# First layer of a vision tower: values projected ahead of keys in the prologue, and the value transfers of the first two tiles issued from two queues

## The reference, cut to what matters

```
h = concat([cls_tok, tok(x)])
n = layernorm(h)
q, k, v = heads(n @ Wq.T) * 16**-0.5, heads(n @ Wk.T), heads(n @ Wv.T)
s = q @ k.T
attn = where(causal, 1 + s + 0.5 * s * s, 0)
h = h + merge(attn @ v / (sum(attn) + 1e-6)) @ Wo.T
```

## Time and profile before

| What | Value |
|---|---|
| Median of 3 runs | 276.23 us |
| Profiled execution | 275.67 us |
| Its span, first to last instruction | 273.9 us |
| PE busy | 240.9 us, 88% |
| PE weight loads busy | 189.0 us, 69% |
| DVE busy | 176.6 us, 64% |
| ACT busy | 135.0 us, 49% |
| POOL busy | 130.3 us, 48% |
| Granted TensorE clock | 1.000 over the whole span |

### The profile page before, as it was taken

How to read it: one execution, slowest core, us unless ns; L and a number is a source line. 1 busy time by engine, 2 the same in 40 slices (tenths; PEclk the granted TensorE clock), 3 DMA queues, 4 the chain that set the end, 5 groups by cost and what they waited for, 6 DMA issues and landing times.

```text
span 273.9 us, 8794 instructions
## 1 busy us (share of the span) xinstructions
PE 240.9 (88%) x3644; PEld 189.0 (69%) x3644; DVE 176.6 (64%) x347; ACT 135.0 (49%) x300; POOL 130.3 (48%) x218
## 2 busy tenths in 40 slices
PE   0779989969999899998897999999999997988983
PEld 0667878857787688887686888789988884443331
DVE  0534537621567899999997998898777776435111
ACT  1322011146576566664455566675766554823450
POOL 7331433561042737565587766878654561154000
PEclk9999999999999999999999999999999999999999
DMA  5989650000111011111100000000000000002021
GB/s 165 221 229 304 131 133 0 4 0 30 47 43 35 31 36 38 35 36 36 33 11 0 2 2 2 2 5 6 2 0 2 5 2 0 4 0 68 2 68 45
DMA packets 12541, 12.44 MB, mean 45 GB/s; under 512 B 4435, under 2 KB 11670, under 8 KB 12502
## 3 DMA queue, kind: packets, MB, share of 16 engines
q1 hardware_dynamic: 12086, 11.88, 15.5%
q10 hardware_dynamic: 416, 0.01, 0.1%
HBM read 8.07 MB, written 1.25 MB: 34 GB/s over the span
## 4 chain that ended last, share of the span: by engine, by line
PE 63%; DVE 18%; issue 7%; DMA 5%; ACT 4%; SPq 2%; DVEq 0%; ACTq 0%
PE psum L1261 12%; PE psum L1297 9%; PE psum L1458 5%; PE psum L1441 5%; DMA img<-in_x 4%; PE psum L1541 3%; PE psum L1604 3%; PE psum L1592 3%; DVE img L1024 3%; PE psum L1516 3%; PE psum L1376 2%; PE psum L1531 2%; PE psum L1233 2%; DVE big L1016 2%; PE psum L1574 2%
## 5 line engine op out<-in xcount | busy, mean ns | idle before, releaser
L481 POOL TENSOR_SCALAR ve<-mvs 114x1 f32<-114x1 f32 x44 | 17.0, 387 | 81.1 <-DVE mvs L979 80.2
L1297 PE MATMUL psum<-hnT,a 128*128 128x114 f32 x352 | 49.0, 282 | 1.1 <-issue 0.6
L1297 PEld LDWEIGHTS psum<-hnT,a 128*128 128x128 f32 x352 | 43.1, 191 | 6.7 <-ACT img L702 2.6
L1261 PE MATMUL psum<-wT,patchT 128*114 128x256 f32 x132 | 33.0, 404 | 1.6 <-DVE patchT L933 0.8
L476 POOL TENSOR_SCALAR big<-mT,parmask 128x228 f32<-128x228 f32 x22 | 22.3, 1026 | 18.4 <-ACT mT L671 18.4
L482 POOL TENSOR_TENSOR rstd<-ve,nhalf 114x1 f32<-114x1 f32 x44 | 28.2, 641 | 3.7
L1261 PEld LDWEIGHTS psum<-wT,patchT 128*114 128x114 f32 x132 | 24.3, 190 | 7.0 <-DVE patchT L933 2.1
L1016 DVE SCALAR_TENSOR_TENSOR big<-big,img 76x912 f32<-76x912 f32 x11 | 15.8, 1438 | 13.1 <-ACT big L727 12.9
L977 DVE BATCH_NORM_STATS2 st<-h_all 114x6 f32<-114x256 f32 x44 | 18.8, 428 | 1.5
L1024 DVE RECIPROCAL img<-img 128x228 f32<-128x228 f32 x11 | 17.3, 1570 | 1.0 <-ACT img L736 1.0
L840 ACT ACTIVATE qc<-psum,b 128x456 f32<-128x456 f32 (+1 forms) x24 | 13.1, 609 | 9.1 <-PE psum L1592 9.1
(11 more groups left out here) (154 smaller groups left out, 513.9 us busy)
## 6 DMA issues: line engine op xcount, KB each, us to landing
img<-in_x SPq DMA_DIRECT2D x6, 576.0 KB, 10.5
img<-vS SPq DMA_DIRECT2D x66, 38.0 KB
out<-h_all SPq DMA_DIRECT2D x10, 114.0 KB
w_raw<-in_L_tok_W SPq DMA_DIRECT2D x1, 768.0 KB, 6.1
a_raw<-in_L_attn_Wq SPq DMA_DIRECT2D x1, 256.0 KB, 8.4
a_raw<-in_L_attn_Wk SPq DMA_DIRECT2D x1, 256.0 KB, 8.5
a_raw<-in_L_attn_Wv SPq DMA_DIRECT2D x1, 256.0 KB, 8.8
a_raw<-in_L_attn_Wo SPq DMA_DIRECT2D x1, 256.0 KB, 12.4
```

Of the source, the lines that this page charges most:

```text
L481: step(nc.gpsimd.tensor_scalar(ve[:, t:t + 1], mvs[:, t, 1:2], LN_EPS, None, ALU.add))
L1261: last = nc.tensor.matmul(EB[t % 2][0:T, 0:D], patchT[:, c, FIRST[t]:FIRST[t] + TI, :].rearrange("p b s -> p (b s)"), wT[:, c, :], start=( ...
L1297: return nc.tensor.matmul(bk[:, m * T:(m + 1) * T], w[:, c, m * 128:(m + 1) * 128], hnT[:, c, :], start=(c == 0), stop=(c == DC - 1))
```

## The change

PE and ACT get another order in the prologue of the first layer. Values of tile 0 are projected and taken ahead of its keys. The turn of tile 1 stands between the keys and the queries of tile 0; the values of tile 1 come right behind the queries of tile 0, ahead of the scores of tile 0 and of the keys of tile 1. On ACT, `norm0(1)` stands behind `take_v0(0)`, and `norm0(2)` behind `square(0)`.

For tiles 0 and 1 SP issues only the transfers of the first half (`o` = 0), three for each tile. The three of the second half are issued by POOL, ahead of its `layer0()`, and count on a pair of new semaphores, `v_moved_first`. The waits for the moved values are adapted. For tiles 2 to 10 SP issues all six as before.

```
@@ sync
-                    for o in range(2):
+                    for o in range(2 if t > 1 else 1):
                         sp.dma_start(vB0[t % 2][o * S:(o + 1) * S, i, :], vS[i * S:(i + 1) * S, t % 2, o * D:(o + 1) * D]
                                      ).then_inc(v_moved[t % 2], 16)
@@ gpsimd
             pool.wait_ge(ld_b, 16)
+            for t in range(2):
+                pool.wait_ge(lay[0]["v_sb"], t + 1)
+                for i in range(TI):
+                    pool.dma_start(vB0[t][S:2 * S, i, :], vS[i * S:(i + 1) * S, t, D:2 * D]).then_inc(v_moved_first[t], 16)
             layer0()
@@ scalar, take_v0
-                ge(act, v_moved[t % 2], 16 * 2 * TI * (t // 2))
+                if t > 1:
+                    act.wait_ge(v_moved[t % 2], 16 * TI * (2 * (t // 2) - 1))
+                    act.wait_ge(v_moved_first[t % 2], 16 * TI)
@@ scalar, layer0
                 norm0(0)
                 take_hnT0(0)
+                take_v0(0)
                 norm0(1)
                 take_k0(0)
-                take_v0(0)
+                take_hnT0(1)
                 take_q0(0)
-                take_hnT0(1)
+                take_v0(1)
+                square(0)
                 norm0(2)
-                square(0)
                 take_k0(1)
-                take_v0(1)
                 take_q0(1)
                 take_hnT0(2)
@@ tensor, values0
-                pe.wait_ge(v_moved[t % 2], 16 * 2 * TI * (t // 2 + 1))
+                pe.wait_ge(v_moved[t % 2], 16 * TI * (2 * (t // 2) + 1))
+                if t < 2:
+                    pe.wait_ge(v_moved_first[t], 16 * TI)
@@ tensor, layer0
                 turn0(0)
+                v_proj0(0)
                 k_proj0(0)
-                v_proj0(0)
+                turn0(1)
                 q_proj0(0)
-                turn0(1)
+                v_proj0(1)
                 scores0(0)
                 k_proj0(1)
-                v_proj0(1)
                 q_proj0(1)
                 turn0(2)
```

More of the change, by code:

```diff
@@ L264, in vit_tower @@
         v_moved = [sem("v_moved0"), sem("v_moved1")]
+        v_moved_first = [sem("v_moved_first0"), sem("v_moved_first1")]
         z_ps = sem("z_ps")
```

## The result

The changed kernel took 280.25 us as the median of 20 executions, the kernel before 276.54 us over 20 beside them. Without the executions that are over 1.5% above the fastest of the same kernel (7 of the 20 here), the ratio is **1.0093, with a 95% interval of 1.0063 to 1.0123**: 0.9% slower, clear of noise and under the 2% that were to count. On the 276.23 us of the kernel before that is 278.8 us, inside the predicted 275.5 to 280.0. The plain median, 280.25, lies just above that range. Run twice more, on two chips, the same kernel gave 1.0036 (1.0002 to 1.0070) and 1.0063 (1.0025 to 1.0101). All three intervals lie above 1.

What follows compares the result with a forecast made beforehand. PE, busy 88% of the span, was taken to bound the kernel. 275.67 + 1.7 us from the order, nothing for the queues, gave 277.4 profiled; that execution lay 0.56 below the median, so 277.9 us, range 275.5 to 280.0.

Steps and rivals of the forecast that it cites:

- the 2% that were to count: Whole kernel: only about 2% (5.5 us) or more can be told from no change; slower by over 2% had 0.07.
- The bound and the 0.37 us: Transfers ahead of values0(0) look like 7 us in the chain but cost PE 0.37 us, the most a faster move returns.
- Part 1, the order: First-layer prologue on PE and ACT: same instructions, new gaps, so values0(0) could start at 71.20 instead of 69.67.
- The gap that was to be the largest: PE idles ahead of q_proj0(1), waiting for take_k0(1) on ACT: 1.29 us.
- +1.53: Predicted delay in us of values0(0), with the 0.37 us of the old transfer wait already taken off.
- The carry to the end: From out_proj0(0) on, everything follows by data, so the delay of +1.7 us lasts to the end.
- +1.71: Predicted delay in us of out_proj0(0), which starts at 75.35 instead of 73.64.
- the rival of a loss that is swallowed: Stalls of 2.3 us in sums0 absorb the later start: 276.2 us, or 275.9 with 0.37 us gained; chance 0.15.
- Part 2, the queues: Transfers of tiles 0 and 1 shared by SP and POOL: worth nothing, 4 us of slack ahead of values0(0).
- The 3.83 us of the earlier trace: Taken as the time from the end of SP's last issue to its landing, in the transfers ahead of values0(0).
- The rule on GpSimd and VectorE: POOL's issues may be held while DVE works, 0.62 us becoming 3.1; expected to touch at most the second three.
- The price outside the span: New queue's fixed cost outside the timeline: taken as 0 of 0 to 1.8 us; rival 0.5 to 1.8, chance 0.10.

Runs made afterwards that it cites:

- The queues alone: Changed kernel with PE and ACT prologues as in the kernel before, transfers shared by SP and POOL: ratio 1.0007, turn0(0) to values0(0) 10.14 us.
- the second run: The changed kernel executed again, unedited, against the kernel before: ratio 1.0036, turn0(0) to values0(0) 12.24 us.
- the early norm: Kernel before with weight_part(0)'s two copies moved from ACT to DVE, so norm0(0) no longer stands behind them: ratio 0.9885, median 273.78 us.
- the filled kernels: Changed kernel with useless matmuls in its two largest PE gaps, 4 and 9 or 2 and 4: ratios 1.0016 and 1.0083 against the kernel before.
- The third run: The changed kernel once more, unedited, on the chip of the control, against the kernel before: ratio 1.0063, turn0(0) to values0(0) 12.24 us.
- order only: Changed kernel with SP issuing all six transfers of tiles 0 and 1 and POOL none: ratio 1.0059 against the kernel before.
- its copy: The kernel before, unedited, run as a control of the comparison: ratio 1.0001, turn0(0) to values0(0) 11.36 us.

## Why the prediction was right

**The bound and the 0.37 us.** Right. The chain of waits put 7 us on the transfers, PE's own list of waits 0.3 us. The queues alone gave 0.37 us.

**Part 1, the order.** Right in its mechanism. Against the second run, whose `turn0(0)` starts 1.06 us later than in the kernel before, the predicted starts, moved by those 1.06 us, are 61.05 for `v_proj0(0)` (measured 61.05), 63.95 for `q_proj0(0)` (63.94), 65.54 for `v_proj0(1)` (65.58), 66.41 for `scores0(0)` (66.63), 69.65 for `q_proj0(1)` (69.86) and 72.26 for `values0(0)` (72.46). The gap that was to be the largest is the largest, released by ACT L707. The single step that was off is the value projection. I took 0.87 us from its start to the next item, from projections that stand behind running matmuls. Behind a wait it took 0.96 and 1.05 us, each instruction group 1.12 instead of 1.03. That is the 0.2 us between +1.53 and the measured +1.73.

**The carry to the end.** I had +1.71 at `out_proj0(0)`; measured from `turn0(0)` it is 16.41 instead of 14.48 us (60.22 to 76.63 and 59.16 to 73.64), that is +1.93. Behind it, to the end, the second run has 200.57 us and the kernel before 200.26, with full clock in both. So nothing is given back: the rival of a loss that is swallowed had 0.15 and is refuted in two directions, by the loss that stays and by the gain of the early norm that stays. The early norm has 200.53. The stall of 1.21 us in `sums0`, on which that rival rested, came along with PE's list: it ends 17.35 us behind `out_proj0(0)` in the kernel before and 17.28 us in the second run. It can go when the list itself is changed, as the filled kernels show, but a later start alone did not shorten it. Whole executions at full clock are 1.6 us apart on the chip of the second run; I had 1.7. The one of the third run, 4 us above its neighbours, is left over.

**Part 2, the queues.** Right that they are worth nothing beside the new order: order only and the changed kernel have the same prologue. I had taken 1 us for an issue of POOL; it is 0.51 to 0.80. The 3.83 us of the earlier trace rows were misread by one issue: they run from the start of SP's sixth issue at 65.69, not from its end, so the transfers had 0.6 us more slack than forecast. POOL was done with its six at 68.93 and with `weight_rest(1)` at 70.12. Predicted were 68.9 and 70.1, to which the later start of 1.06 us has to be added, so it was a microsecond quicker than forecast.

**The rule on GpSimd and VectorE.** The direction was the other one. No issue was held up; DVE's masking, 1.10 us alone, took 2.33 us beside `weight_rest(1)`. The Trainium skill ("SBUF — State Buffer", the section on two separate sides) says that the two share a port that is locked for a whole instruction. The trace agrees: the masking ended at 71.09, 0.97 us behind the end of `weight_rest(1)`, about what it takes alone, although its own record begins 0.19 us ahead of that instruction's. The third run and the first profiled execution of the changed kernel have the same 0.97 us; in the latter POOL's issues were over before the masking began, so it is `weight_rest(1)` that holds it. With the order alone `weight_rest(1)` is over long before, and the masking takes 1.10 us. An issue stretched by DVE, which is what the page's 3.1 us would be, no run here shows: the six took 0.51 to 0.80 us each, and their data landed 2.0 to 3.4 us behind. In the changed order PE needs the masked weights only at 72.46, so the 1.2 us cost nothing.

**The price outside the span.** None: 278.96 - 277.2 = 1.8 us in the second run, as before (275.67 - 273.9).

**What was missing.** The forecast had no term for the clock. It is the likely reason why the first comparison came to 0.9% and not to the 0.6% of 1.7 us, but not a shown one: the clocks of the kernel before in that comparison are not on record. In that group no execution of the changed kernel had a mean clock above 0.994. The profiled one was at half clock for 20 us from 60 us on. That fall begins where PE has waited 1.81 us for `hn`, ahead of the gaps that the change makes. The kernel before has the same wait, and the same fall was caught in its copy, for 3 us. What stays open is whether the new order makes it last longer. Filling the gaps gave no executions at full clock; the second and third profiles had no fall there; no run told the two apart.

## What to carry to other kernels

A chain of waits that runs through a transfer doesn't price the transfer. Read what the engine at its end did meanwhile, and how long it idled just ahead of the item that the transfer released; here 0.37 of 7 us. When projections share one bank, the work that doesn't go through it is what covers the copies out of it: moved ahead to start something sooner, it leaves them bare. And an edit of half a per cent is better read off the stretch that it touches, at known clock, than off whole executions; then look once at the stretches behind it, where stalls of 1.5 us together came and went with a few matmuls more.

## What the runs showed of the hardware

- TensorE's granted clock fell to half for 3 to 20 us in kernels with the old order and with the new one: at 12 to 26, at about 60 us, at 90 to 98, at 107 to 112, at 128 to 133 and at 151 to 162 us. Ahead of the fall at 60 us PE had waited 1.81 us; in all five traces with a fall at 90 to 98 us it begins within some 1 us of a stall of 0.93 to 1.22 us in `sums0`; and PE was busy for 3.25 of the 5 us in which the one at 153 us begins. The same idle stretches stand in the traces at full clock, so they are not enough for a fall. Mean clocks of the kernel before ran from 0.963 to 1.000, with times of 273.9 to 282.3 us. A fall at 13 to 24 us, while the images are loaded, costs little: in the copy of the kernel before it did not make `turn0(0)` late (58.83 against 59.16).
- DMA issues of POOL took 0.51 us, the first of a group 0.80, against SP's 0.58 to 0.68 us. The data of POOL's landed 2.2 us behind the start of the issue at the median, three to a group; the last of SP's six took 3.83 us. The two aren't the same place in a row, and the landings of SP's other transfers are not in the traces, so which queue is quicker stays open.
- DVE's masking and POOL's `weight_rest(1)` don't run side by side: where they met, the masking ended 0.97 us behind it and took 1.60 to 2.40 us instead of 1.10.
